# An LSTM step with the output gate's sigmoid apart, the first half's f·c apart, and ScalarE's scale factor held in a register

## The chip, the cores and the metric

One core of one Trainium2 chip runs the kernel. The time is the device time of one execution in microseconds (us). 2701.34 us is the median of three runs of the kernel before.

## The reference

A residual LSTM over 32 sequences of 512 steps, with 512 inputs and 512 hidden units. `Wx` and `Wh` are 512 x 2048, the bias has 2048 values, and all of it is float32:

```python
xW = jnp.einsum('ntd,dg->ntg', x, Wx) + b
c0 = jnp.zeros_like(h0)

def step(carry, xw_t):
    prev_h, prev_c = carry
    a = xw_t + prev_h @ Wh
    i = jax.nn.sigmoid(a[:, :Hd])
    f = jax.nn.sigmoid(a[:, Hd:2 * Hd])
    o = jax.nn.sigmoid(a[:, 2 * Hd:3 * Hd])
    g = jnp.tanh(a[:, 3 * Hd:])
    next_c = f * prev_c + i * g
    next_h = o * jnp.tanh(next_c)
    return ((next_h, next_c), next_h)
```

The output is x + h, for all steps. `x @ Wx` can be computed ahead of its step; `prev_h @ Wh` cannot, since it needs the h of the step before.

## The kernel before, in words

**Layout.** The batch of 32 and the four quarters of the hidden units together fill the 128 partitions: partition 32 j + b holds sequence b and the 128 hidden units of quarter j. A step's four gates for one partition are 512 values: i, f, o, g with 128 each. They are collected in one PSUM bank, `Z[s]`, where s is the step's place in a block of four. One matmul of TensorE has 32 stationary columns; four of them, one for each quarter j, run side by side in the array and fill the 128 partitions, so matmuls come in groups of four.

**Numbers.** Operands are cut into a high and a low float16 part, each scaled by a power of two. A product is then high x high, high x low and low x high. So Z comes out scaled by a factor that changes from block to block, and the gate functions undo that: they compute f(scale * Z) with `z_unscale`, one float32 that is the same in all partitions (column 3 of the tile `scales[:, r]`, made by VectorE in `scale_block`, L626).

**The input part** is computed two steps at a time, by a scheme that needs seven products where eight would be the plain number. TensorE does three and a half of these in each step (`third_products` and `first_product` in even steps, `second_products` and `last_product` in odd ones), six groups of 256 columns to a product, hence 21 groups a step. ScalarE and VectorE prepare the operands and move partial sums (`take_p5`, `set_c21`, `set_c11`, `cut_x_hi`, `set_c12`, `set_run`, `set_extra` on ScalarE; `add_extra`, `cut_x_lo`, `turn_x`, the forms, `scale_block` on VectorE).

**The recurrent part** (`recurrent_part`, L383) is 12 groups of 512 columns: first those of the high part of h, chunks 0 and 1 once `hT_hi_done` says that the first half of h is there, chunks 2 and 3 with the second half, then those of the low part once `hT_lo_done` says so. Its last matmul raises `z_done`.

**Order on TensorE** (L399): the recurrent part of step t, then the 21 groups of input products for later steps, then the recurrent part of t+1. While TensorE does the 21 groups, ScalarE and VectorE turn Z into the new h:

- ScalarE, `step` (L493): for each half a of the 128 hidden units of a partition, one sigmoid over i, f and o (L499, 3 x 64 values) and one tanh over g (L501, 64 values); then for each half, once c is there, tanh of c (L505). All gate functions take `z_unscale`, a 128 x 1 tile, as their scale, except in step 0, whose Z is not scaled: there the scale is the constant 1.0.
- VectorE, `step` (L751): `products(t, 0)` (L745: i g and f c of the first half in one instruction over 2 x 64 values, for which c and tanh g stand side by side in the tile `gc`), `new_c(t, 0)` (L749), `products(t, 1)`, `high_part_of_h(t, 0)` (L733: o * h_scale * tanh c), `new_c(t, 1)`, `turn_high_part(t, 0)` (L738, a transposition that writes `hT_hi`), `high_part_of_h(t, 1)`, `turn_high_part(t, 1)`. Then h in float32 (L763), the low part of h (L765) and its transposition (L768), the output sum (L775), and the work for later input products.

Each engine works through its own list in the order written; semaphores tie the lists together, and nothing reorders them. Once a block, at the end of s = 3, ScalarE copies the next block's factor into `z_unscale` (`set_z_unscale`, L489, copy in L491). SP issues all loads and stores; POOL only shares the maximum of x over partitions (L816).

There are 128 blocks of four steps. Blocks 0 and 1 and the last six are written out in the lists of ScalarE, VectorE, POOL and SP, with a loop over pairs of blocks between them; TensorE loops over single blocks. In the last steps the input products run out, since no later steps need them.

Of the kernel before, what the change touches and what calls it, by code (L numbers as in the profile page):

```python
# [6 lines left out]
F32 = mybir.dt.float32  # L7
# [3 lines left out]
ALU = mybir.AluOpType  # L11
ACT = mybir.ActivationFunctionType
# [3 lines left out]
def lstm_residual(nc, x, h0, Wx, Wh, bias, out):  # L16
# [12 lines left out]
    P = 128  # L29
    NJ = H // P  # L30
    C = P
# [18 lines left out]
    with ctx:  # L50
        def sb(name, shape, dt=F32):
            return ctx.enter_context(nc.sbuf_tensor(name, shape, dt))

        def bank(name):
            return ctx.enter_context(nc.psum_tensor(name, [P, 512], F32))

        def sem(name):
            return ctx.enter_context(nc.semaphore(name))
# [27 lines left out]
        act = sb("act", [P, ZW])  # L86

        gc = sb("gc", [P, 2, 2, C // 2])
        igfc = sb("igfc", [P, 2, 2, C // 2])
# [24 lines left out]

        scales = sb("scales", [P, 2, 4], I32)
        h_scale = sb("h_scale", [P, 1])
        z_unscale = sb("z_unscale", [P, 1])


        Z = [bank(f"Z{s}") for s in range(TB)]  # L120
# [34 lines left out]
        xfield_n_done = sem("xfield_n_done")  # L155
        zs_done = sem("zs_done")
        scales_done = sem("scales_done")
        h_scale_set = sem("h_scale_set")
        z_unscale_set = sem("z_unscale_set")
        x_turned = sem("x_turned")  # L160
# [25 lines left out]

        z_done = sem("z_done")
        sig_done = sem("sig_done")
        tanh_g_done = sem("tanh_g_done")
        igfc_done = sem("igfc_done")  # L190
        c_done = sem("c_done")
        tanh_c_done = sem("tanh_c_done")
# [19 lines left out]
        def half(tile, a):  # L212
            return tile[:, a * HC:(a + 1) * HC]

        def half_gates(tile, a):
            return tile.rearrange("p (g a c) -> p a g c", g=4, a=2)[:, a]
# [29 lines left out]
        def started(value):  # L246
            return not isinstance(value, int) or value > 0
# [183 lines left out]
        def _(sc):  # L431
# [50 lines left out]
            def take_p5(q, e):  # L482
# [3 lines left out]
                    sc.wait_ge(c22_set, q - 1)  # L486
                nc.scalar.copy(p5[:, :], extra[e][:, 0:HW]).then_inc(p5_taken, 1)

            def set_z_unscale(n, r):  # L489
                sc.wait_ge(scales_done, n + 1)  # L490
                nc.scalar.copy(z_unscale[:, :], scales[:, r, 3:4].bitcast(F32)).then_inc(z_unscale_set, 1)  # L491

            def step(t, n, s):  # L493
                if s == 0:
                    sc.wait_ge(z_unscale_set, n + 1)
                scale = 1.0 if isinstance(t, int) and t == 0 else z_unscale[:, :]
                sc.wait_ge(z_done, t + 1)
                for a in range(2):
                    nc.scalar.activation(half_gates(act, a)[:, 0:3], half_gates(Z[s], a)[:, 0:3],  # L499
                                         ACT.Sigmoid, scale=scale).then_inc(sig_done, 1)  # L500
                    nc.scalar.activation(gc[:, a, 0], half_gates(Z[s], a)[:, 3],  # L501
                                         ACT.Tanh, scale=scale).then_inc(tanh_g_done, 1)
                for a in range(2):
                    sc.wait_ge(c_done, 2 * t + 1 + a)
                    nc.scalar.activation(half(tanh_c, a), gc[:, a, 1], ACT.Tanh).then_inc(tanh_c_done, 1)  # L505
# [40 lines left out]
            set_run(2, 0, 1)  # L546
            set_extra(2, 0, 1)
            set_z_unscale(0, 0)

            def block(i, n, r):  # L550
                for s in range(TB):
                    step(n * TB + s, n, s)
                    if s == 0:
                        if within(2 * n + 1, NQ):
# [22 lines left out]
                    if s == 3:  # L577
                        if within(2 * n + 4, NQ):
                            cut_x_hi(2 * n + 4, n + 2, r, 0)
                        if within(2 * n + 3, NQ):  # L580
                            set_c12(2 * n + 3, 1)
                        if within(2 * n + 4, NQ):
                            set_run(2 * n + 4, 0, r)
                            set_extra(2 * n + 4, 0, r)
                        if within(n + 1, NB):
                            set_z_unscale(n + 1, 1 - r)
# [4 lines left out]
        def _(v):  # L591
# [109 lines left out]
            def prepare():  # L701
                nc.vector.memset(gc[:, :, 1], 0.0).then_inc(c_cleared, 1)
                turn_x(0, 0, 1)
                v.wait_ge(bias_loaded, 16 * NJ)
                nc.vector.tensor_tensor(bias_d[:, :], bias_bc[:, HW:], bias_bc[:, 0:HW], ALU.subtract).then_inc(bias_d_done, 1)
                turn_x(1, 1, 1)
                weight_scale(0)
                v.wait_ge(h0_loaded, 16 * NJ)
                nc.vector.transpose(h0_T[:, :, :], h0_in[:, :].rearrange("p (ch l) -> p ch l", ch=NCH)).then_inc(h0_turned, 1)
                for place, (k, _) in enumerate(W_ORDER):  # L710
                    cut_wx_lo(k, place)
                weight_scale(1)
                scale_tables()
                scale_block(0, 0)
                scale_block(1, 1)
                set_h_scale(0, 0)
                first_forms(0, 0)
                last_forms(0, 0)
                cut_wh_lo(0)
                cut_x_lo(1, 0, 1)  # L720
                cut_wh_lo(1)
                first_forms(1, 1)
                last_forms(1, 1)
                cut_wh_lo(2)
                cut_wh_lo(3)
                turn_x(2, 0, 2)

                cut_x_lo(2, 1, 0)
                scale_block(2, 0)

            def high_part_of_h(t, a):
                v.wait_ge(tanh_c_done, 2 * t + 1 + a)
                nc.vector.scalar_tensor_tensor(half(h_hi, a), half_gates(act, a)[:, 2], h_scale[:, :], half(tanh_c, a),  # L733
                                               ALU.mult, ALU.mult).then_inc(h_hi_done, 1)

            def turn_high_part(t, a):
                v.wait_ge(h_hi_done, 2 * t + 1 + a)
                nc.vector.transpose(hT_hi[:, NCH // 2 * a:NCH // 2 * (a + 1), :],  # L738
                                    half(h_hi, a).rearrange("p (ch l) -> p ch l", l=L)).then_inc(hT_hi_done, 1)

            def products(t, a):

                v.wait_ge(sig_done, 2 * t + 1 + a)
                v.wait_ge(tanh_g_done, 2 * t + 1 + a)
                nc.vector.tensor_tensor(igfc[:, a], half_gates(act, a)[:, 0:2], gc[:, a], ALU.mult).then_inc(igfc_done, 1)  # L745

            def new_c(t, a):
                v.wait_ge(igfc_done, 2 * t + 1 + a)
                nc.vector.tensor_tensor(gc[:, a, 1], igfc[:, a, 1], igfc[:, a, 0], ALU.add).then_inc(c_done, 1)  # L749

            def step(t):  # L751
                products(t, 0)
                new_c(t, 0)
                products(t, 1)
                high_part_of_h(t, 0)
                new_c(t, 1)
                turn_high_part(t, 0)
                high_part_of_h(t, 1)
                turn_high_part(t, 1)
                if started(t):  # L760

                    v.wait_ge(y_done, t)
                nc.vector.tensor_tensor(h32[:, :], act[:, 2 * C:3 * C], tanh_c[:, :], ALU.mult).then_inc(h32_done, 1)  # L763
                v.wait_ge(h32_done, t + 1)
                nc.vector.scalar_tensor_tensor(h_lo[:, :], h32[:, :], h_scale[:, :], h_hi[:, :],  # L765
                                               ALU.mult, ALU.subtract).then_inc(h_lo_done, 1)
                v.wait_ge(h_lo_done, t + 1)
                nc.vector.transpose(hT_lo[:, :, :], h_lo[:, :].rearrange("p (ch l) -> p ch l", ch=NCH)).then_inc(hT_lo_done, 1)  # L768
# [90 lines left out]
```

## Time and profile before

| | us |
|---|---|
| runs (3) | 2698.51, 2701.34, 2701.63; median 2701.34 |
| the profiled execution, its time | 2700.78 |
| its span, first to last instruction | 2699.0 |
| TensorE matmuls busy | 2611.6 (97%) |
| VectorE busy | 2150.0 (80%) |
| ScalarE busy | 1694.0 (63%) |
| POOL busy | 72.4 (3%) |
| mean granted TensorE clock, share of full speed | 0.988 |

What lies outside of the span is 1.8 us. The profiled execution is 0.56 us faster than the median of the three runs. Matmul ends are modelled in such a profile and neighbouring matmuls overlap, so TensorE's 97% is not to be taken as 97% at its peak; the starts of the groups say more.

### The profile page before, as it was taken

The page shows a single profiled execution, that of the slowest core. Times are in us where ns is not written, and L with a number is a line of the kernel's source. Part 1 is how long each engine was busy: PE and PEld are TensorE (multiplying, and loading weights), DVE is VectorE, ACT ScalarE, POOL GpSimd, SP SyncE. Part 2 cuts the span into 40 slices and gives each one's busy share as a digit, 9 for nine tenths or more (in the row PEclk, how much of TensorE's full clock was granted, in tenths as well). Part 3 has the DMA queues.
Part 4 walks back from the last instruction along what each step waited for, and adds up shares of the span by engine and source line. Part 5 has one row for each costly group of instructions (what it writes and reads, how often), then busy time and mean ns, then how long its engine had stood idle before and what let it go on. Part 6 is the DMA issues. An engine that isn't in the chain of part 4 may idle for free.

```text
span 2699.0 us, 163151 instructions
## 1 busy us (share of the span) xinstructions
PE 2611.6 (97%) x67528; PEld 1755.8 (65%) x67528; DVE 2150.0 (80%) x8259; ACT 1694.0 (63%) x5392; POOL 72.4 (3%) x138
## 2 busy tenths in 40 slices
PE   3599999999999999999999999999999999999998
PEld 0366666666666666666666666666666666666665
DVE  4888888888888888888888888888888888888876
ACT  2566666666666666666666666666666666666664
POOL 3000000000000000000000000000000000000000
PEclk7799999999999999999999999999999999999999
DMA  6011111111111111111111111111111111111111
GB/s 149 18 40 43 35 39 43 35 39 43 35 39 43 35 39 43 35 39 43 35 39 43 35 39 43 35 39 43 35 38 43 35 39 43 35 39 43 35 35 25
DMA packets 223517, 109.85 MB, mean 41 GB/s; under 512 B 25216, under 2 KB 222464, under 8 KB 222464
## 3 DMA queue, kind: packets, MB, share of 16 engines
q1 hardware_dynamic: 223488, 109.48, 16.2%
q8 instruction: 16, 0.26, 0.0%
q14 instruction: 13, 0.11, 0.0%
HBM read 75.83 MB, written 33.55 MB: 41 GB/s over the span
## 4 chain that ended last, share of the span: by engine, by line
PE 95%; DVE 1%; ACT 1%; issue 0%; DVEq 0%; ACTq 0%
PE Z L318 71%; PE run L318 18%; PE extra L318 6%; DVE wh_lo L681 0%; DVE gc L749 0%; ACT act L499 0%; DVE igfc L745 0%; DVE h_hi L733 0%; ACT tanh_c L505 0%; ACT wh_hi L524 0%; ACT gc L501 0%; DVE hT_hi L738 0%; DVE x_lo L615 0%; DVE zs L634 0%; DVE h_lo L765 0%
## 5 line engine op out<-in xcount | busy, mean ns | idle before, releaser
L318 PE MATMUL Z<-wh_hi,hT_hi 128*32 128x512 f16 x8176 | 801.5, 382 | 7.6 <-DVE hT_hi L738 6.4
L499 ACT ACTIVATE act<-Z,z_unscale 128x192 f32<-128x192 f32 x1022 | 431.1, 422 | 583.0 <-PE Z L318 583.0
L318 PE MATMUL Z<-wh_lo,hT_hi 128*32 128x512 f16 x8176 | 796.2, 379 | 0.0
L318 PE MATMUL Z<-wh_hi,hT_lo 128*32 128x512 f16 x8176 | 529.7, 379 | 0.0
L745 DVE TENSOR_TENSOR igfc<-act,gc 128x128 f32<-128x128 f32 x1024 | 299.6, 293 | 285.0 <-ACT gc L501 284.6
L318 PE MATMUL run<-wx_hi,x_hi 128*32 128x256 f16 x6120 | 433.1, 273 | 44.5 <-DVE x_lo L615 42.3
L505 ACT ACTIVATE tanh_c<-gc 128x64 f32<-128x64 f32 x1024 | 262.4, 256 | 339.3 <-DVE gc L749 339.3
L318 PEld LDWEIGHTS Z<-wh_hi,hT_hi 128*32 128x32 f16 x8176 | 214.6, 95 | 352.1 <-DVE hT_hi L738 234.8
L318 PE MATMUL run<-wx_lo,x_hi 128*32 128x256 f16 x6120 | 433.2, 273 | 0.0
L318 PE MATMUL run<-wx_hi,x_lo 128*32 128x256 f16 x6120 | 433.2, 273 | 0.0
L318 PE MATMUL Z<-wx_lo,x_hi 128*32 128x256 f16 x6120 | 432.8, 273 | 0.0
L318 PE MATMUL Z<-wx_hi,x_lo 128*32 128x256 f16 x6120 | 432.8, 273 | 0.0
L318 PE MATMUL Z<-wx_hi,x_hi 128*32 128x256 f16 x6120 | 432.8, 273 | 0.0
L733 DVE SCALAR_TENSOR_TENSOR h_hi<-act,h_scale,tanh_c 128x64 f16<-128x64 f32 x1024 | 291.8, 285 | 120.2 <-ACT tanh_c L505 85.9
L318 PEld LDWEIGHTS Z<-wh_hi,hT_lo 128*32 128x32 f16 x8176 | 215.4, 96 | 225.8 <-DVE hT_lo L768 113.5
L501 ACT ACTIVATE gc<-Z,z_unscale 128x64 f32<-128x64 f32 x1022 | 322.3, 315 | 0.0
L318 PEld LDWEIGHTS Z<-wh_lo,hT_hi 128*32 128x32 f16 x8176 | 218.4, 97 | 133.0 <-issue 0.7
L738 DVE STREAM_TRANSPOSE hT_hi<-h_hi 128x64 f16<-128x64 f16 x1024 | 247.6, 242 | 17.8
L749 DVE TENSOR_TENSOR gc<-igfc 128x64 f32<-128x64 f32 x1024 | 226.9, 222 | 17.4
L318 PEld LDWEIGHTS run<-wx_hi,x_hi 128*32 128x32 f16 x6120 | 164.1, 97 | 104.2 <-issue 41.6
L318 PEld LDWEIGHTS run<-wx_lo,x_hi 128*32 128x32 f16 x6120 | 164.1, 97 | 57.5
L765 DVE SCALAR_TENSOR_TENSOR h_lo<-h,h_scale,h_hi 128x128 f16<-128x128 f32 x512 | 180.3, 352 | 18.1
(88 smaller groups left out, 3586.6 us busy)
## 6 DMA issues: line engine op xcount, KB each, us to landing
x_in<-in_x SPq DMA_DIRECT2D x512, 64.0 KB, 2.1
x_res<-in_x SPq DMA_DIRECT2D x512, 64.0 KB, 2.1
out_y<-y SPq DMA_DIRECT2D x512, 64.0 KB, 1.7
wx_raw<-in_Wx SPq DMA_DIRECT2D x16, 256.0 KB, 9.1
wh_raw<-in_Wh SPq DMA_DIRECT2D x16, 256.0 KB, 20.0
bias_bc<-in_bias SPq DMA_DIRECT2D x4, 64.0 KB, 2.1
h_in<-in_h SPq DMA_DIRECT2D x4, 16.0 KB, 14.1
```

The source lines that it names most:

```text
L318: return nc.tensor.matmul(out, lhsT, rhs, start=False, stop=last, skip_group_check=True)
L499: nc.scalar.activation(half_gates(act, a)[:, 0:3], half_gates(Z[s], a)[:, 0:3], ACT.Sigmoid, scale=scale).then_inc(sig_done, 1)
L501: nc.scalar.activation(gc[:, a, 0], half_gates(Z[s], a)[:, 3], ACT.Tanh, scale=scale).then_inc(tanh_g_done, 1)
L505: nc.scalar.activation(half(tanh_c, a), gc[:, a, 1], ACT.Tanh).then_inc(tanh_c_done, 1)
L733: nc.vector.scalar_tensor_tensor(half(h_hi, a), half_gates(act, a)[:, 2], h_scale[:, :], half(tanh_c, a), ALU.mult, ALU.mult).then_inc(h_h ...
L738: nc.vector.transpose(hT_hi[:, NCH // 2 * a:NCH // 2 * (a + 1), :], half(h_hi, a).rearrange("p (ch l) -> p ch l", l=L)).then_inc(hT_hi_don ...
L745: nc.vector.tensor_tensor(igfc[:, a], half_gates(act, a)[:, 0:2], gc[:, a], ALU.mult).then_inc(igfc_done, 1)
L749: nc.vector.tensor_tensor(gc[:, a, 1], igfc[:, a, 1], igfc[:, a, 0], ALU.add).then_inc(c_done, 1)
L765: nc.vector.scalar_tensor_tensor(h_lo[:, :], h32[:, :], h_scale[:, :], h_hi[:, :], ALU.mult, ALU.subtract).then_inc(h_lo_done, 1)
```

## The change

ScalarE's sigmoid over i, f and o of a half becomes one over i and f alone (2 x 64 values). The sigmoid of o is one instruction over both halves (128 values) behind the four others, with a semaphore of its own, `sig_o_done`, that VectorE waits for ahead of the first `high_part_of_h`. On VectorE, i g and f c of the first half become two instructions: f c waits for the sigmoid alone, i g for the tanh of g. The second half stays as it was. The tile `z_unscale` becomes a register of ScalarE, loaded once a block from partition 0 of `scales`; the gate functions name the register as their scale.

```diff
@@ semaphores @@
+        scales_seen = sem("scales_seen")
...
+        sig_o_done = sem("sig_o_done")
...
+        fc_done = sem("fc_done")
+        ig_done = sem("ig_done")
@@ ScalarE @@
+            z_unscale = sc.alloc_register("z_unscale")
+
             def set_z_unscale(n, r):
                 sc.wait_ge(scales_done, n + 1)
-                nc.scalar.copy(z_unscale[:, :], scales[:, r, 3:4].bitcast(F32)).then_inc(z_unscale_set, 1)
+                sc.sem_inc(scales_seen, 1)
+                sc.reg_load(z_unscale, scales[0:1, r, 3:4]).then_inc(z_unscale_set, 1)
 
             def step(t, n, s):
-                if s == 0:
-                    sc.wait_ge(z_unscale_set, n + 1)
-                scale = 1.0 if isinstance(t, int) and t == 0 else z_unscale[:, :]
+                scale = 1.0 if isinstance(t, int) and t == 0 else z_unscale
                 sc.wait_ge(z_done, t + 1)
                 for a in range(2):
-                    nc.scalar.activation(half_gates(act, a)[:, 0:3], half_gates(Z[s], a)[:, 0:3],
+                    nc.scalar.activation(half_gates(act, a)[:, 0:2], half_gates(Z[s], a)[:, 0:2],
                                          ACT.Sigmoid, scale=scale).then_inc(sig_done, 1)
                     nc.scalar.activation(gc[:, a, 0], half_gates(Z[s], a)[:, 3],
                                          ACT.Tanh, scale=scale).then_inc(tanh_g_done, 1)
+
+                nc.scalar.activation(act[:, 2 * C:3 * C], Z[s][:, 2 * C:3 * C],
+                                     ACT.Sigmoid, scale=scale).then_inc(sig_o_done, 1)
@@ VectorE @@
             def high_part_of_h(t, a):
+                if a == 0:
+                    v.wait_ge(sig_o_done, t + 1)
                 v.wait_ge(tanh_c_done, 2 * t + 1 + a)
...
-            def products(t, a):
...
-            def new_c(t, a):
...
+            def first_products(t):
+
+                v.wait_ge(sig_done, 2 * t + 1)
+                nc.vector.tensor_tensor(igfc[:, 0, 1], half_gates(act, 0)[:, 1], gc[:, 0, 1], ALU.mult).then_inc(fc_done, 1)
+                v.wait_ge(tanh_g_done, 2 * t + 1)
+                nc.vector.tensor_tensor(igfc[:, 0, 0], half_gates(act, 0)[:, 0], gc[:, 0, 0], ALU.mult).then_inc(ig_done, 1)
+
+            def first_c(t):
+                v.wait_ge(fc_done, t + 1)
+                v.wait_ge(ig_done, t + 1)
+                nc.vector.tensor_tensor(gc[:, 0, 1], igfc[:, 0, 1], igfc[:, 0, 0], ALU.add).then_inc(c_done, 1)
+
+            def last_products(t):
+
+                v.wait_ge(sig_done, 2 * t + 2)
+                v.wait_ge(tanh_g_done, 2 * t + 2)
+                nc.vector.tensor_tensor(igfc[:, 1], half_gates(act, 1)[:, 0:2], gc[:, 1], ALU.mult).then_inc(igfc_done, 1)
+
+            def last_c(t):
+                v.wait_ge(igfc_done, t + 1)
+                nc.vector.tensor_tensor(gc[:, 1, 1], igfc[:, 1, 1], igfc[:, 1, 0], ALU.add).then_inc(c_done, 1)
 
             def step(t):
-                products(t, 0)
-                new_c(t, 0)
-                products(t, 1)
+                first_products(t)
+                first_c(t)
+                last_products(t)
                 high_part_of_h(t, 0)
-                new_c(t, 1)
+                last_c(t)
                 turn_high_part(t, 0)
```

## Rows read from the trace of the kernel before

**Rows 1.** The page's first part: busy us, share of span and instructions of each engine
```profile
PE 2611.6 (97%) x67528; PEld 1755.8 (65%) x67528; DVE 2150.0 (80%) x8259; ACT 1694.0 (63%) x5392; POOL 72.4 (3%) x138
```
**Rows 2.** Critical chain in order of time, two pieces: start us, us, what
```profile
161.30 3.42 PE Z L318 x72
...
2560.35 3.42 PE Z L318 x72
```
**Rows 3.** Timeline, TensorE, one step: start us, us, engine, line, op, out<-in, count
```profile
1300.79 0.40 PE L318 MATMUL Z<-wh_hi,hT_hi 128*32 128x512 f16 x4
...
1303.39 0.28 PE L318 MATMUL run<-wx_hi,x_hi 128*32 128x256 f16 x4
...
1305.57 0.28 PE L318 MATMUL Z<-wx_hi,x_lo 128*32 128x256 f16 x4
...
1305.85 0.40 PE L318 MATMUL Z<-wh_hi,hT_hi 128*32 128x512 f16 x4
```
**Rows 4.** Waits, longest in total: engine, line, waited for, us in total, times, longest
```profile
PEld Z L318 <- DVE hT_hi L738: 234.8, 1010, 2.8
```
**Rows 5.** Timeline, ScalarE and VectorE, the chain between two recurrent parts
```profile
1303.62 0.42 ACT L499 ACTIVATE act<-Z,z_unscale 128x192 f32<-128x192 f32 x1 [1.29 <-PE Z L318]
...
1303.93 0.31 ACT L501 ACTIVATE gc<-Z,z_unscale 128x64 f32<-128x64 f32 x1
...
1304.34 0.29 DVE L745 TENSOR_TENSOR igfc<-act,gc 128x128 f32<-128x128 f32 x1 [0.73 <-ACT gc L501]
...
1304.67 0.23 DVE L749 TENSOR_TENSOR gc<-igfc 128x64 f32<-128x64 f32 x1
...
1304.93 0.26 ACT L505 ACTIVATE tanh_c<-gc 128x64 f32<-128x64 f32 x1 [0.17 <-DVE gc L749]
...
1305.22 0.28 DVE L733 SCALAR_TENSOR_TENSOR h_hi<-act,h_scale,tanh_c 128x64 f16<-128x64 f32 x1
...
1305.56 0.24 DVE L738 STREAM_TRANSPOSE hT_hi<-h_hi 128x64 f16<-128x64 f16 x1
```
**Rows 6.** Timeline, weight loads for h's second high half and its low part
```profile
1306.58 0.10 PEld L318 LDWEIGHTS Z<-wh_hi,hT_hi 128*32 128x32 f16 x4 [0.18 <-DVE hT_hi L738]
...
1307.49 0.64 PEld L318 LDWEIGHTS Z<-wh_hi,hT_lo 128*32 128x32 f16 x16 [0.23 <-DVE hT_lo L768]
```
**Rows 7.** Timeline, ScalarE in step 0, whose scale is the constant 1.0
```profile
101.33 0.33 ACT L499 ACTIVATE act<-Z 128x192 f32<-128x192 f32 x1
101.55 0.22 ACT L501 ACTIVATE gc<-Z 128x64 f32<-128x64 f32 x1
101.66 0.34 ACT L499 ACTIVATE act<-Z 128x192 f32<-128x192 f32 x1
```
**Rows 8.** Timeline, VectorE in step 0: two instructions that wait for nothing
```profile
103.48 0.22 DVE L749 TENSOR_TENSOR gc<-igfc 128x64 f32<-128x64 f32 x1
103.62 0.28 DVE L745 TENSOR_TENSOR igfc<-act,gc 128x128 f32<-128x128 f32 x1
```
**Rows 9.** Timeline, ScalarE in a step with s = 3, and the next step's start
```profile
1293.50 0.42 ACT L499 ACTIVATE act<-Z,z_unscale 128x192 f32<-128x192 f32 x1 [1.29 <-PE Z L318]
...
1295.85 0.63 ACT L458 ACTIVATE x_hi<-forms 128x512 f16<-128x512 f32 x1
...
1297.09 0.46 ACT L468 ACTIVATE extra<-bias_d,scales 128x256 f32<-128x256 f32 x1
1297.49 0.17 ACT L491 COPY z_unscale<-scales 128x1 f32<-128x1 f32 x1
1298.56 0.42 ACT L499 ACTIVATE act<-Z,z_unscale 128x192 f32<-128x192 f32 x1 [0.89 <-PE Z L318]
```
**Rows 10.** Timeline, VectorE: its last instruction of the same step
```profile
1298.69 0.22 DVE L640 SCALAR_TENSOR_TENSOR scales<-scale_mul,zs,scale_add 128x4 int32<-128x4 int32 x1
```
**Rows 11.** DMA issues: issue line, count, KB each, us to landing
```profile
x_in<-in_x SPq DMA_DIRECT2D x512, 64.0 KB, 2.1
...
out_y<-y SPq DMA_DIRECT2D x512, 64.0 KB, 1.7
```
**Rows 12.** Timeline, TensorE in the last step, with no input products left
```profile
2688.63 0.40 PE L318 MATMUL Z<-wh_hi,hT_hi 128*32 128x512 f16 x4 [2.28 <-DVE hT_hi L738]
```

More of the change, by code:

```diff
@@ L116, in lstm_residual @@
         h_scale = sb("h_scale", [P, 1])
-        z_unscale = sb("z_unscale", [P, 1])
         Z = [bank(f"Z{s}") for s in range(TB)]
@@ L739, in turn_high_part @@
                                     half(h_hi, a).rearrange("p (ch l) -> p ch l", l=L)).then_inc(hT_hi_done, 1)
-            def products(t, a):
-                v.wait_ge(sig_done, 2 * t + 1 + a)
-                v.wait_ge(tanh_g_done, 2 * t + 1 + a)
-                nc.vector.tensor_tensor(igfc[:, a], half_gates(act, a)[:, 0:2], gc[:, a], ALU.mult).then_inc(igfc_done, 1)
-            def new_c(t, a):
-                v.wait_ge(igfc_done, 2 * t + 1 + a)
-                nc.vector.tensor_tensor(gc[:, a, 1], igfc[:, a, 1], igfc[:, a, 0], ALU.add).then_inc(c_done, 1)
+            def first_products(t):
[14 more added lines that the diff above has]
+                nc.vector.tensor_tensor(gc[:, 1, 1], igfc[:, 1, 1], igfc[:, 1, 0], ALU.add).then_inc(c_done, 1)
             def step(t):
-                products(t, 0)
-                new_c(t, 0)
-                products(t, 1)
+                first_products(t)
+                first_c(t)
+                last_products(t)
                 high_part_of_h(t, 0)
-                new_c(t, 1)
+                last_c(t)
                 turn_high_part(t, 0)
```

## The prediction

> **What bounds the kernel now.** The page's first part comes first: TensorE shows 97% busy, VectorE 80%, ScalarE 63% [rows 1], which looks as if only less matmul work could help. The critical chain in order of time gives the beat: from 161.30 to 2560.35 us lie 474 steps, so one step takes 2399.05 / 474 = 5.061 us, without drift [rows 2]. The third view, the timeline of one step, shows what fills this beat, by starts and not by ends. The recurrent part starts at 1300.79 and the input products at 1303.39, 2.60 us for its 12 groups. The 21st group of products starts at 1305.57, hence 2.18 / 20 = 0.109 us a group, and the last is through its turn at 1305.68. The next recurrent part starts at 1305.85 [rows 3]. So TensorE stands still for 0.17 us in each step: 2.60 + 2.29 + 0.17 = 5.06. The model of the matmul ends hides this hole, but the waits name what ends it: the weight load of the recurrent part waits for the transposed first half of h, 1010 times in the sum for both halves [rows 4].
>
> So the beat is a loop of latencies: Z complete, gate functions, c, tanh c, high part of h, its transposition, and TensorE's 12 groups again. Counted from ScalarE's start at 1303.62 [rows 5]: tanh of g ends at 0.62, the products start at 0.72, c at 1.05, tanh c at 1.31, h_hi at 1.60, the transposition at 1.94, and the recurrent part at 2.23. From there to ScalarE's next start are the other 2.83 of the 5.06 us (12 groups, the last one's end, the signal). A microsecond saved in the 2.23 shortens the step until TensorE's own 2.60 + 2.29 = **4.89 us** bounds it, and no further.
>
> Does the second half, or the low part, hold the loop instead? Their weight loads take 0.10 us each and start just in time for the next group [rows 6]; they have next to no slack, but they follow h_hi of the first half in VectorE's order at fixed distances. What comes earlier ahead of that h_hi brings them forward by as much.
>
> **The register as scale.** No row shows a scale from a register. The nearest rows bound it: a scale from a 128 x 1 tile (0.42 us for 192 values, 0.31 for 64 [rows 5]) and the constant of step 0 (0.33 and 0.22 [rows 7]), 0.09 less. Starts also follow closer: 0.32 behind the 192 values with the tile, 0.22 with the constant, and 0.11 behind the 64. I take the constant's value, since a register, like a constant, needs no read of 128 partitions, and these are rows of the same instructions. The tile's price stays as the other end. The Trainium skill (ScalarE: Activation LUTs, What ACT_TABLE_LOAD costs) says that immediate scale and bias take 186 ns + 0.833 ns a value and each pointer operand some 93 ns more; the trace agrees (0.09 us, and (0.33 - 0.22) / 128 = 0.86 ns a value), but neither page nor trace has the register's case. By the rule the constant's sum below would hold if the register counts as an immediate.
>
> **The sigmoid over i and f alone** spares 64 x 0.86 ns = 0.05 us ahead of the tanh of g. With the constant's durations: first sigmoid 0 to 0.28; tanh of g from 0.17 to 0.40 (0.62 before).
>
> **f c apart.** An instruction of VectorE with one wait starts 0.03 us behind what it waits for (h_hi behind tanh c), one with two waits of which the second comes last 0.10 (the products behind tanh g) [rows 5]. f c has one: it starts at 0.31. Two independent instructions, the first of 64 values, start 0.14 apart [rows 8], so i g starts at 0.45 (tanh g would allow 0.43). It takes 0.22, as c's sum over 64 values does [rows 5], where both products together took 0.29; it ends at 0.67. The sum for c now has two waits: 0.77 to 0.99. Tanh c: 1.02 to 1.28.
>
> **Sigmoid of o behind.** ScalarE's five starts are 0.17, 0.11, 0.17, 0.11 and 0.17 apart, so it is free for tanh c at 0.73, and o is there at 0.56 + 0.28 = 0.84; both are early. h_hi has two waits now: 1.28 + 0.10 = 1.38, where it was 1.60. **The loop is 0.22 us shorter**: 4.84. The second half's products need VectorE from about 0.87 on for 0.29 us, done before 1.38. What was paid for the extra waits (0.07 twice) and f c's own instruction is in this sum.
>
> TensorE's 4.89 is longer than 4.84, by a thin 0.05. **So TensorE bounds the step, and each full step gives back 0.17 of the 0.22.**
>
> **What else must keep up.** ScalarE with s = 3: x_hi starts 2.35 us behind the step's start, when TensorE's products end (their last group starts at 1305.57, 1.95 behind ScalarE's start, and takes 0.28 [rows 3, 5]), and the last copy ends at 1297.55, 4.05 behind the start [rows 9]. This part hangs on TensorE and doesn't come earlier. The register load must fit between 4.05 and 4.89, 0.84 us; what is queued behind it is the next step's first sigmoid, and behind that everything. Nothing in the trace is a register load: below it is bounded by the copy that it replaces, 0.17 us [rows 9], above by a DMA, 1.7 to 2.1 us to its landing [rows 11]. I take it as covered, because it reads one word that lies in the core's own memory, as the copy does, and no 64 KB. The Trainium skill (DMA: Bandwidth & Descriptors, Latency and other measured facts) gives a tensor_load a floor of about 600 ns, which would fit; the same skill (Runtime: NRT & Kernel Launch, the preamble breakdown) has about 1.3 us for register loads from HBM, which would not: by it 0.46 us would stand out. No run here shows either.
>
> VectorE with s = 3 has its longest list: L640 starts at 1298.69, 3.59 behind that step's h_hi and 0.13 behind the next step's start [rows 9, 10]. It comes at 1.38 + 3.59 = 4.97 of a step of 4.89, so at 0.08 of the next, and f c is wanted at 0.31: covered. SP and POOL get nothing new; the stores hang on y, which comes earlier with the step.
>
> **The sum.** 502 full steps x 0.17 = 85.3. In the last six or so the products thin out, TensorE waits up to 2.28 us for h [rows 12], and each gets the whole 0.22: 1.3. Together 86.6, less something for the loop branch of TensorE, of which no row was read: 86. Against the profiled execution's own 2700.8 that gives 2615 us; the median of the runs shown is 0.6 higher, so a median might be 2615.5. **Predicted: 2615 us**, 3.2% less.
>
> **The rivals.**
> *The register costs what the tile did.* Then tanh of g ends at 0.27 + 0.31 = 0.58, i g at 0.83, c at 1.15; but five starts (0.27 and 0.20 apart, the tile's 0.32 less 0.05 and the constant's 0.11 with 0.09 more) keep ScalarE busy to 1.21, and o's sigmoid becomes the wait ahead of tanh c. h_hi starts at 1.57, 0.03 earlier: 15 us, 2685. For it: the instruction form is unseen. Against: nothing must be fetched from 128 partitions. 6%.
> *Some of the price only.* A few hundredths for each of five gate functions, or a wait dearer than counted, and the loop of 4.84 rises over 4.89; 0.05 more costs 25 us beyond the slack. 2630 to 2655, around 2640. 12%, for the slack is thin.
> *The load holds ScalarE* (the slower side). Place: the end of s = 3, in front of the next block's first sigmoid. It costs (load - 0.84) for 127 blocks; from 0.84 + 86 / 127 = 1.52 us on the kernel is slower than before. At a DMA's 2.1 us: 1.26 x 127 = 160, hence 2775. For it: a DMA needs that long. Against: one word, no queue. 5%. At 1.3 us by the page named above it would be 0.46 x 127 = 58, 2673; 4%.
> *The floor is lower or the hole isn't there.* The hole could belong to TensorE's own change from products to the recurrent part, and then nothing is gained: 2700. The waits speak against it [rows 4]. 3%. The forecast keeps 70%.
>
> **How the numbers follow.** The forecast's own range is 2604 (0.19 us a step, if the first group of the recurrent part loses its late weight load as well) to 2629 (0.14). To hold 8 in 10 the range takes in the partial price: 2604 to 2655. What a measurement of this kernel can tell from no change is 0.2%, 5.4 us. Faster by more than that: forecast, partial price, tile's price, load at 1.3 us, 0.92. Same: 0.03. Slower: 0.05.
>
> **What would show it.** Right: a step of 4.89 us over hundreds of steps; gate functions at 0.28 (128 values) and 0.22; h_hi 1.38 behind the sigmoid's start; the products' last group and the recurrent part 0.11 apart; PEld waiting less for hT_hi. Wrong: gate functions at 0.37 and 0.31, tanh c waiting for nothing but ScalarE's own queue; a step of s = 0 longer than the others, with ScalarE idle between L468 and the sigmoid and TensorE waiting behind it; or a step of 4.89 that TensorE spends with a hole in it.

## The result, and the profile after

The changed kernel takes **2627.91 us** (median of 4 runs, 2626.70 to 2628.84) against 2700.64 for the kernel before (also 4 runs). The ratio is 0.9731, with a 95% interval of 0.9715 to 0.9748: 72.7 us less. The forecast was 2615, within 2604 to 2655.

The page of the changed kernel, busy time of each engine, the counterpart of [rows 1] (PE is TensorE, PEld its weight loads, DVE VectorE, ACT ScalarE):

```profile
PE 2534.0 (97%) x67528; PEld 1769.6 (67%) x67528; DVE 2176.8 (83%) x8771; ACT 1528.8 (58%) x5776; POOL 72.4 (3%) x138
```

TensorE does the same 67528 matmuls, and its share still reads 97%: this number was as blind to the hole as to its closing. The wait that ended the hole is the better witness. The waits of the changed kernel, the counterpart of [rows 4]:

```profile
PEld Z L321 <- DVE hT_hi L747: 62.4, 251, 2.6
```

234.8 us in 1010 waits became 62.4 in 251. In the timeline of TensorE, one plain step of the changed kernel shows it directly (counterpart of [rows 3]):

```profile
1301.07 0.39 PE L321 MATMUL Z<-wh_hi,hT_hi 128*32 128x512 f16 x4
...
1305.84 0.28 PE L321 MATMUL run<-wx_hi,x_lo 128*32 128x256 f16 x4
1305.95 0.39 PE L321 MATMUL Z<-wh_hi,hT_hi 128*32 128x512 f16 x4
```

The last group of products and the recurrent part are 0.11 us apart, one group's turn, where they were 0.28. The step is 4.88 us (the seven from 577.33 to 611.52, below, take 34.19). The chain in between, ScalarE and VectorE of the same step (counterpart of [rows 5]):

```profile
1303.88 0.28 ACT L503 ACTIVATE act<-Z 128x128 f32<-128x128 f32 x1 [0.83 <-PE Z L321]
1304.06 0.22 ACT L505 ACTIVATE gc<-Z 128x64 f32<-128x64 f32 x1
...
1304.92 0.26 ACT L512 ACTIVATE tanh_c<-gc 128x64 f32<-128x64 f32 x1 [0.18 <-DVE gc L760]
...
1304.01 0.22 DVE L647 SCALAR_TENSOR_TENSOR scales<-scale_mul,zs,scale_add 128x4 int32<-128x4 int32 x1
1304.20 0.23 DVE L753 TENSOR_TENSOR igfc<-act,gc 128x64 f32<-128x64 f32 x1
1304.34 0.22 DVE L755 TENSOR_TENSOR igfc<-act,gc 128x64 f32<-128x64 f32 x1
1304.66 0.23 DVE L760 TENSOR_TENSOR gc<-igfc 128x64 f32<-128x64 f32 x1
...
1305.28 0.29 DVE L742 SCALAR_TENSOR_TENSOR h_hi<-act,h_scale,tanh_c 128x64 f16<-128x64 f32 x1
```

The gate functions have the constant's durations, 0.28 and 0.22, and h_hi starts 1.40 us behind the first sigmoid, 1.60 before; 1.38 was forecast.

Some 505 steps (half of the 1010 waits of [rows 4]) at 0.178 less would give 90 us, more than the 72.7 measured. What is missing lies in one step of eight. The same engines around 614 us, where the loop of VectorE turns over:

```profile
614.34 0.28 ACT L503 ACTIVATE act<-Z 128x128 f32<-128x128 f32 x1 [0.84 <-PE Z L321]
...
614.48 0.22 DVE L647 SCALAR_TENSOR_TENSOR scales<-scale_mul,zs,scale_add 128x4 int32<-128x4 int32 x1
615.01 0.23 DVE L753 TENSOR_TENSOR igfc<-act,gc 128x64 f32<-128x64 f32 x1 [0.32 <-ACT act L503]
...
615.48 0.23 DVE L760 TENSOR_TENSOR gc<-igfc 128x64 f32<-128x64 f32 x1
...
616.10 0.28 DVE L742 SCALAR_TENSOR_TENSOR h_hi<-act,h_scale,tanh_c 128x64 f16<-128x64 f32 x1
```

From the start of L647 to that of f c (L753) are 0.53 us here and 0.19 in the plain case above, which is the same place in the other block of the loop; there f c waits for the sigmoid and not for L647. The idle time here is put down to the sigmoid too, but that ended at 614.62. What stands between is seen only in the view of the loop's own line, L261, in this stretch (DVEq is VectorE's sequencer; number, shortest/median/longest in ns, first and last start):

```profile
L261 DVEq COMPARE_BRANCH x1: 56/56/56, 614.6 to 614.6; - x1
L261 DVEq FUSED_REGOPS x1: 85/85/85, 614.9 to 614.9; - x1
```

The sequencer branches back and computes its registers, with 0.3 us from the one's start to the other's; what fills that time is in no view. f c starts 0.67 us behind the first sigmoid instead of 0.31. h_hi comes at 1.76, and TensorE waits. Its recurrent parts there:

```profile
577.33 0.40 PE L321 MATMUL Z<-wh_hi,hT_hi 128*32 128x512 f16 x4
...
611.52 0.40 PE L321 MATMUL Z<-wh_hi,hT_hi 128*32 128x512 f16 x4
...
616.73 0.40 PE L321 MATMUL Z<-wh_hi,hT_hi 128*32 128x512 f16 x4
```

The last two are 5.21 us apart, and the eight steps from 577.33 to 616.73 take 39.40, 0.34 more than 8 x 4.883. 60 loop turns of that are some 20 us, as read from the trace; the run with the branch moved, below, measures 16.8.

### The profile page after: what moved, and what is told of

It reads as the page before. It is cut to its first block, busy times and chain, and to the rows that moved or that the text cites. A ratio compares the mean times of both kernels' runs of the same rounds, so it can differ in the third digit from the quotient of the medians.

```text
span 2625.3 us, 164755 instructions
## 1 busy us (share of the span) xinstructions
PE 2534.0 (97%) x67528; PEld 1769.6 (67%) x67528; DVE 2176.8 (83%) x8771; ACT 1528.8 (58%) x5776; POOL 72.4 (3%) x138
## 4 chain that ended last, share of the span: by engine, by line
PE 68%; DVE 20%; issue 4%; ACT 4%; DVEq 1%; ACTq 0%
PE Z L321 53%; PE run L321 12%; PE extra L321 4%; DVE h_hi L742 3%; ACT tanh_c L512 3%; DVE h_lo L786 2%; DVE gc L760 2%; DVE igfc L755 2%; DVE hT_hi L747 2%; DVE x_lo L622 1%; DVE y L796 1%; DVE gc L770 1%; DVE igfc L753 1%; DVE h L784 1%; DVE Z L628 1%
## 5 line engine op out<-in xcount | busy, mean ns | idle before, releaser
L503 ACT ACTIVATE act<-Z 128x128 f32<-128x128 f32 x1024 | 287.2, 281 | 558.4 <-PE Z L321 558.4
L321 PEld LDWEIGHTS Z<-wh_hi,hT_hi 128*32 128x32 f16 x8176 | 214.7, 95 | 256.0 <-DVE hT_hi L747 62.4
L505 ACT ACTIVATE gc<-Z 128x64 f32<-128x64 f32 x1024 | 235.9, 230 | 0.0
L753 DVE TENSOR_TENSOR igfc<-act,gc 128x64 f32<-128x64 f32 x512 | 115.6, 226 | 109.2 <-ACT act L503 93.6
L461 ACT ACTIVATE x_hi<-forms 128x512 f16<-128x512 f32 x255 | 160.6, 630 | 58.1 <-PE Z L321 58.1
```

Of the source, the lines that this page charges most:

```text
L321: return nc.tensor.matmul(out, lhsT, rhs, start=False, stop=last, skip_group_check=True)
L461: nc.scalar.activation(x_hi[:, e], forms_of_pair(r, e), ACT.Copy).then_inc(x_hi_cut, 1)
L503: nc.scalar.activation(half_gates(act, a)[:, 0:2], half_gates(Z[s], a)[:, 0:2], ACT.Sigmoid, scale=scale).then_inc(sig_done, 1)
L753: nc.vector.tensor_tensor(igfc[:, 0, 1], half_gates(act, 0)[:, 1], gc[:, 0, 1], ALU.mult).then_inc(fc_done, 1)
```

## The experiments

Times are compared with the kernel before, run beside each group of experiments (medians of 2699.8 to 2701.6 us), or with the changed kernel's 2627.9.

**The scale back in the tile.** In the changed kernel:

```diff
-            z_unscale = sc.alloc_register("z_unscale")
+        z_unscale = sb("z_unscale", [P, 1])
...
-                sc.reg_load(z_unscale, scales[0:1, r, 3:4]).then_inc(z_unscale_set, 1)
+                nc.scalar.copy(z_unscale[:, :], scales[:, r, 3:4].bitcast(F32)).then_inc(z_unscale_set, 1)
...
-                scale = 1.0 if isinstance(t, int) and t == 0 else z_unscale
+                scale = 1.0 if isinstance(t, int) and t == 0 else z_unscale[:, :]
```

> The changed kernel with its scale factor in the 128 x 1 tile again. Theory A (the register is what brings the gain, since gate functions of 128 values drop from 0.37 to 0.28 us and the queue of five from 1.21 to 0.73 us; the two splits alone bring 0.03 us a step): tanh c waits for ScalarE's own queue, h_hi starts near 1.57 us behind the first sigmoid, a step takes 5.03 us and every eighth one some 0.2 us more, in all about 2695 us, no more than 15 us below the kernel before. Theory B (the splits bring at least half of the gain): 2665 us or less.

Measured: 2685.77 us (2684.70 to 2687.53), ratio 0.9946 (0.9931 to 0.9961). Theory A. Its timeline, ScalarE and VectorE:

```profile
1301.91 0.37 ACT L502 ACTIVATE act<-Z,z_unscale 128x128 f32<-128x128 f32 x1 [0.95 <-PE Z L321]
1302.18 0.31 ACT L504 ACTIVATE gc<-Z,z_unscale 128x64 f32<-128x64 f32 x1
...
1302.82 0.39 ACT L507 ACTIVATE act<-Z,z_unscale 128x128 f32<-128x128 f32 x1
1303.11 0.26 ACT L511 ACTIVATE tanh_c<-gc 128x64 f32<-128x64 f32 x1
...
1303.47 0.28 DVE L741 SCALAR_TENSOR_TENSOR h_hi<-act,h_scale,tanh_c 128x64 f16<-128x64 f32 x1
```

Tanh c (L511) has no idle time ahead of it: ScalarE's queue holds it, at 1.20 us, and h_hi comes at 1.56. A plain step takes 5.01 us, somewhat less than expected, and the step at the loop branch 5.21. With the tile the two splits are worth 15 us, and the register on top of them the other 58. That holds for this order alone: the next run takes the register first.

**The register alone.** In the kernel before, the register in place of the tile and nothing else (the first diff read the other way round):

> The kernel before with the register as scale and nothing else changed. Theory A: tanh of g ends 0.44 us behind the first sigmoid's start, the products start at 0.54, h_hi at 1.41; the loop of 4.87 us is under TensorE's own 4.883, so TensorE bounds the step here too. At VectorE's loop branch, once in eight steps, the products start near 0.73 and the step is 0.2 us longer (60 times, 12 us). About 2617 us, some 10 us below the changed kernel. Theory B (each part of the change adds to the gain): clearly over 2628 us, 2645 or more.

Measured: 2619.53 us (2617.88 to 2619.84), ratio 0.9701 (0.9688 to 0.9715). Theory A, and less than the whole change takes. Its timeline at VectorE's loop branch:

```profile
612.10 0.33 ACT L500 ACTIVATE act<-Z 128x192 f32<-128x192 f32 x1 [0.83 <-PE Z L318]
...
612.84 0.29 DVE L746 TENSOR_TENSOR igfc<-act,gc 128x128 f32<-128x128 f32 x1 [0.39 <-ACT act L500]
...
613.71 0.28 DVE L734 SCALAR_TENSOR_TENSOR h_hi<-act,h_scale,tanh_c 128x64 f16<-128x64 f32 x1
```

The branch holds this kernel too, its products starting at 0.74, but from there to h_hi are 0.87 us, against 1.09 from f c to h_hi in the changed kernel: there is no second product instruction, one wait less ahead of the sum, and one less ahead of h_hi. The eight steps to the recurrent part behind it take 39.24 us (575.10 to 614.34), so the long one is 5.06 if the other seven are at TensorE's 4.883.

**The branch moved.** In the changed kernel, VectorE's loop is cut behind the work of s = 0, and the instructions on data and their order stay:

```diff
-            def block(i, n, r):
-                for s in range(TB):
+            def block(i, n, r, steps=range(4)):
+                for s in steps:
...
-            run_blocks(v, block)
+            last = NB // BODY
+            block(0, 0, 0)
+            block(0, 1, 1)
+            block(1, 2, 0, (0,))
+            with v.Fori(1, last - 3) as i:
+                block(i, i * BODY, 0, (1, 2, 3))
+                block(i, i * BODY + 1, 1)
+                block(i + 1, i * BODY + 2, 0, (0,))
+            block(last - 3, (last - 3) * BODY, 0, (1, 2, 3))
+            block(last - 3, (last - 3) * BODY + 1, 1)
+            for i in range(last - 2, last):
+                for r in range(BODY):
+                    block(i, i * BODY + r, r)
```

> The changed kernel with VectorE's loop cut at another place: its branch stands behind the work of a step with s = 0 (the shortest list) in place of s = 3 (the longest). No instruction on data is added or taken away. Theory A (the eighth step of 5.20 us is VectorE's branch, which puts f c 0.67 us behind the first sigmoid's start where 0.31 was wanted): all steps take 4.88 us, 60 x 0.31 = 19 us less, 2609 us. Rival (the long step belongs to ScalarE's branch, to the register load or to TensorE's own loop): the long step stays, 2628 us.

Measured: 2611.06 us (2609.93 to 2611.39), ratio 0.9668 (0.9655 to 0.9681). Theory A. Eight recurrent parts on TensorE, with the loop's turn among them:

```profile
600.72 0.39 PE L321 MATMUL Z<-wh_hi,hT_hi 128*32 128x512 f16 x4
...
639.81 0.39 PE L321 MATMUL Z<-wh_hi,hT_hi 128*32 128x512 f16 x4
```

39.09 us, 4.886 a step. The long step is gone, and the 16.8 us between this kernel and the changed one are shown to be the branch's place. Of the 20 us read from the trace 2 are not won, since a step here is still 0.003 over 4.883; the rest is within what the runs scatter.

**The branch moved in the kernel before.** The same edit there, as a control:

> The kernel before with VectorE's loop branch behind the work of s = 0, and nothing else. Theory A (the branch cost nothing before the change, since the first products were wanted 0.72 us behind the sigmoid's start and the branch let them go at 0.70): the steps stay at 5.06 us and the time within 2 us of the kernel before. Rival (the branch cost time in the kernel before too): 10 to 19 us less.

Measured: 2700.33 us (2699.22 to 2701.15), ratio 0.9999 (0.9990 to 1.0009). Theory A. The branch cost nothing that can be measured before the change; it was covered by the very latency that the register took away.

**Both products of the first half whole again.** In the changed kernel:

```diff
                 v.wait_ge(sig_done, 2 * t + 1)
-                nc.vector.tensor_tensor(igfc[:, 0, 1], half_gates(act, 0)[:, 1], gc[:, 0, 1], ALU.mult).then_inc(fc_done, 1)
                 v.wait_ge(tanh_g_done, 2 * t + 1)
-                nc.vector.tensor_tensor(igfc[:, 0, 0], half_gates(act, 0)[:, 0], gc[:, 0, 0], ALU.mult).then_inc(ig_done, 1)
+                nc.vector.tensor_tensor(igfc[:, 0], half_gates(act, 0)[:, 0:2], gc[:, 0], ALU.mult).then_inc(ig_done, 1)
...
-                v.wait_ge(fc_done, t + 1)
```

> The changed kernel with i g and f c of the first half in one instruction again (128 values, waiting for sigmoid and tanh), o and the register as changed. Theory A: products at 0.49 us, c at 0.81 against 0.78 with f c apart (the sum for c has one wait again), h_hi at 1.42; the loop of 4.88 us is at TensorE's 4.883, nothing is lost in a plain step. At VectorE's branch one instruction less stands between it and c: c near 1.03 in place of 1.13, so that the long step shrinks by 0.1 us, 60 x 0.1 = 6 us: 2622 us. Rival (f c apart carries its 0.07 us in full): a step of 4.93 us, 2645 to 2650 us.

Measured: 2635.28 us (2633.70 to 2636.88), ratio 0.9759 (0.9745 to 0.9772). Neither. Theory A had the sign wrong: without f c apart the kernel loses 7 us where it was to win 6. The plain step is 4.893, so the loop of latencies is now 0.01 us over TensorE's floor, some 5 us in all: h_hi comes at 1.44 and not at the 1.42 expected. The step at the branch is 5.14, 0.06 less than in the changed kernel, where 0.1 was expected. And one step in eight, away from the branch, takes 4.99. ScalarE and VectorE in that step:

```profile
588.19 0.28 ACT L502 ACTIVATE act<-Z 128x128 f32<-128x128 f32 x1 [0.84 <-PE Z L320]
...
588.78 0.29 DVE L753 TENSOR_TENSOR igfc<-act,gc 128x128 f32<-128x128 f32 x1 [0.43 <-ACT act L502]
```

The products start 0.59 us behind the sigmoid and not at 0.49, with VectorE idle. What holds them for that 0.1 us (6 us in all) stays open; no run was made for it.

**The sigmoid of o back with i and f**, f c apart and the register as changed:

```diff
-                    nc.scalar.activation(half_gates(act, a)[:, 0:2], half_gates(Z[s], a)[:, 0:2],
+                    nc.scalar.activation(half_gates(act, a)[:, 0:3], half_gates(Z[s], a)[:, 0:3],
                                          ACT.Sigmoid, scale=scale).then_inc(sig_done, 1)
...
-                nc.scalar.activation(act[:, 2 * C:3 * C], Z[s][:, 2 * C:3 * C],
-                                     ACT.Sigmoid, scale=scale).then_inc(sig_o_done, 1)
...
-                if a == 0:
-                    v.wait_ge(sig_o_done, t + 1)
```

> The changed kernel with the sigmoid of o back in those of i and f (192 values), so that h_hi waits for tanh c alone; f c apart and the register as changed. Theory A: in a plain step nothing changes, 4.883 us, since TensorE bounds it. At VectorE's branch the front of the chain is given by the branch, and h_hi starts 0.03 us behind tanh c in place of 0.10, so the long step shrinks from 5.20 to 5.13 us: 60 x 0.07 = 4 us, 2624 us. Rival (o behind carries its 0.05 us ahead of tanh g in the long step too): 5.20 us or more, 2628 us or more.

Measured: 2620.76 us (2619.55 to 2621.22), ratio 0.9706 (0.9692 to 0.9719). Theory A in sign, and twice its size: eight steps take 39.26 us (575.75 to 615.01), so the long one is 5.08 and not 5.13. The split of o costs 7 us where it stands. The branch in this run:

```profile
612.75 0.33 ACT L502 ACTIVATE act<-Z 128x192 f32<-128x192 f32 x1 [0.83 <-PE Z L320]
...
612.83 0.22 DVE L643 SCALAR_TENSOR_TENSOR scales<-scale_mul,zs,scale_add 128x4 int32<-128x4 int32 x1
613.37 0.23 DVE L747 TENSOR_TENSOR igfc<-act,gc 128x64 f32<-128x64 f32 x1 [0.31 <-ACT act L502]
...
614.38 0.28 DVE L736 SCALAR_TENSOR_TENSOR h_hi<-act,h_scale,tanh_c 128x64 f16<-128x64 f32 x1
```

From f c to h_hi are 1.01 us, 0.08 less than in the changed kernel. And f c itself starts 0.62 us behind its sigmoid, where the changed kernel has 0.67. These 0.05 come from the step before, whose h_hi starts VectorE's list down to the branch. First the changed kernel's, then this run's:

```profile
609.46 0.28 ACT L503 ACTIVATE act<-Z 128x128 f32<-128x128 f32 x1 [1.33 <-PE Z L321]
...
610.89 0.28 DVE L742 SCALAR_TENSOR_TENSOR h_hi<-act,h_scale,tanh_c 128x64 f16<-128x64 f32 x1
```

```profile
607.87 0.33 ACT L502 ACTIVATE act<-Z 128x192 f32<-128x192 f32 x1 [1.34 <-PE Z L320]
...
609.25 0.29 DVE L736 SCALAR_TENSOR_TENSOR h_hi<-act,h_scale,tanh_c 128x64 f16<-128x64 f32 x1
```

h_hi comes 1.43 us behind the sigmoid there and 1.38 here, and from it to L647 or L643 are 3.59 and 3.58.

**The register alone, with the branch moved:**

> The register alone, with VectorE's loop branch behind the work of s = 0, as in the run with the branch moved. Theory A (TensorE bounds every step once the branch is out of the way, and neither split of the change is then needed): all steps 4.883 us, the eighth 0.17 us shorter than with the register alone, 60 x 0.17 = 10 us less than 2619.5, so 2609 us, the same as the changed kernel with the branch moved (2611) within 3 us. Rival (the splits still carry something, as the loop of 4.88 us with the products whole is at TensorE's 4.883): 2615 us or more.

Measured: 2608.97 us (2606.96 to 2612.18), ratio 0.9664 (0.9651 to 0.9677). Theory A. This is the lowest median of the study (single runs overlap with those of the changed kernel with its branch moved), with one instruction less a step than the changed one on VectorE and one less on ScalarE. From

```profile
599.61 0.39 PE L318 MATMUL Z<-wh_hi,hT_hi 128*32 128x512 f16 x4
...
638.67 0.39 PE L318 MATMUL Z<-wh_hi,hT_hi 128*32 128x512 f16 x4
```

eight steps take 39.06 us, 4.883 each. TensorE bounds every one.

**What the register load costs.** Two kernels tried to repeat it. Six loads of the one register in a row:

> The changed kernel with six loads of the register in a row in place of one. One load showed 0.28 us and stood in the trace beside copies that are ahead of it in ScalarE's program. Theory A (loads pass beside the work that is queued, from about 2.5 us behind a step's start on, and six take some 2.1 us, which end before the next step): no change, 2628 us, at most 5 more. Rival (a load waits its turn behind the last copy, at 4.05 us, with 0.84 us of room): six take 2.1 us, 1.26 us too long, 127 times, 2785 us.

Measured: 2629.56 us (2627.73 to 2629.68). That tells nothing: the trace holds 128 loads, one a block, as the changed kernel's does. Loads whose value was overwritten before use were no longer in the program. The same with a signal behind each load:

> Six loads of the register in a row again, each with its own signal now, since only one load a block stood in the trace of the run before it. Theory A (loads pass beside the queued work, and six of 0.28 us with some 0.07 between them take 2.1 us from 2.5 us behind the step's start, 4.6 in a step of 4.88): no more than 5 us over the changed kernel's 2628. Rival (a load waits behind the last copy at 4.05 us): 1.26 us too long, 127 times, 2785 us.

Measured: 2636.11 us (2635.26 to 2638.12), 8 us over the changed kernel, and again 128 loads; the other five became signals alone, so it tells nothing of loads either. (Its step at the branch is 5.32 us. VectorE's wait for the register, which counts six a block now, was changed with it; that this makes the 0.12 us wasn't tried.) What remained was to use every load: five registers, one for each gate function of a step.

```diff
-            z_unscale = sc.alloc_register("z_unscale")
+            z_unscale = [sc.alloc_register(f"z_unscale{k}") for k in range(5)]
...
-                sc.reg_load(z_unscale, scales[0:1, r, 3:4]).then_inc(z_unscale_set, 1)
+                for reg in z_unscale:
+                    load = sc.reg_load(reg, scales[0:1, r, 3:4])
+                load.then_inc(z_unscale_set, 1)
...
-                                         ACT.Sigmoid, scale=scale).then_inc(sig_done, 1)
+                                         ACT.Sigmoid, scale=scale[2 * a]).then_inc(sig_done, 1)
```

> The changed kernel with a register of its own for each of the five gate functions of a step, so that each block needs five loads that are all used. Theory A (loads pass beside the queued work from 2.5 us behind the step's start, 0.35 us each, 1.75 in all, done at 4.3 of 4.88): within 5 us of the changed kernel's 2628. Rival (loads wait behind the last copy, room 0.84 us): 0.91 us too long, 127 times, 2743 us.

Measured: 2630.27 us (2627.38 to 2631.70), within 2.4 us of the changed kernel. Theory A. The trace has 640 loads, five a block.

> The same with ten registers, five for even and five for odd steps. Theory A: ten loads of 0.35 us take 3.5 us from 2.5 on and end at 6.0, 1.1 us into the next step: 127 times 1.1 us more, 2770 us. Rival (loads wait behind the last copy): 2.7 us too long, 127 times, 2965 us.

Measured: 2751.44 us (2749.89 to 2752.89), ratio 1.0187 (1.0170 to 1.0204). Theory A, with the loads shorter than assumed. The view of the load's line in one block of it, then ScalarE around it and the recurrent parts on either side:

```profile
L498 ACTq TENSOR_LOAD <-scales x10: 273/276/436, 1299.1 to 1302.1; - x10
```

```profile
1296.56 0.28 ACT L506 ACTIVATE act<-Z 128x128 f32<-128x128 f32 x1 [1.33 <-PE Z L321]
...
1299.45 0.37 ACT L479 COPY Z<-run 128x256 f32<-128x256 f32 x1
...
1300.16 0.46 ACT L471 ACTIVATE extra<-bias_d,scales 128x256 f32<-128x256 f32 x1
1302.84 0.28 ACT L506 ACTIVATE act<-Z 128x128 f32<-128x128 f32 x1 [2.22 <-issue]
```

```profile
1298.63 0.40 PE L321 MATMUL Z<-wh_hi,hT_hi 128*32 128x512 f16 x4
...
1304.86 0.40 PE L321 MATMUL Z<-wh_hi,hT_hi 128*32 128x512 f16 x4 [1.16 <-DVE hT_hi L750]
```

The first load starts at 1299.1, ahead of the starts of three instructions that stand before it in the program (L479, L466 and L471); they go on beside the loads. The last ends at some 1302.4, and the next sigmoid, whose input had been ready, starts at 1302.84, with 2.22 us of idle time put down to "issue". Between the two stands ScalarE's own loop branch, which is covered in the changed kernel:

```profile
L261 ACTq COMPARE_BRANCH x1: 45/45/45, 1302.5 to 1302.5; - x1
L261 ACTq FUSED_REGOPS x1: 59/59/59, 1302.7 to 1302.7; - x1
```

The step lasts 6.23 us instead of the changed kernel's 5.2. In a block without the branch it is 5.82 (1319.52 to 1325.34 for the recurrent part) instead of 4.89. In the changed kernel the one load looks like this:

```profile
L497 ACTq TENSOR_LOAD <-scales x1: 276/276/276, 1301.5 to 1301.5; - x1
```

0.28 us, over at 1301.8, and the next sigmoid starts at 1303.88: 2.1 us to spare.

## Why the prediction was right, and where it was 13 us off

**The bound.** Right: a loop of latencies with a hole of 0.17 us on TensorE, and a floor of 4.89 (4.883 measured: the first recurrent group no longer starts behind a late weight load). The recurrent part itself takes 2.59 us in the timeline of the changed kernel (1301.07 to the products' start at 1303.66), 2.60 before. The kernel with register and moved branch sits on this floor in every step.

**The register as scale.** Right, and it is the step that everything hung on: 0.28 and 0.22 us, the constant's price, and 2619.5 us by this edit alone. The first rival, the tile's price, was put at 2685 us; the run with the tile took 2685.8. This agreement is partly luck, since a plain step gained 0.05 there and not 0.03, and the branch took some of it back.

**The two splits.** Their sum was right in a plain step (h_hi at 1.38 forecast, 1.40 measured), but they were not asked separately whether they were needed. By the prediction's own method the register alone gives h_hi at 1.41 or 1.42 and a loop under the floor; the splits then buy slack that nobody uses in a plain step.

**What else must keep up.** This is the step that failed: "It comes at 1.38 + 3.59 = 4.97 of a step of 4.89, so at 0.08 of the next, and f c is wanted at 0.31: covered." VectorE's list was followed to L640, its last instruction on data, and not over the loop branch behind it. The instruction comes at 0.14 of the next step and not at 0.08, since h_hi of the step before is at 1.43 and not at 1.38, which alone would have cost nothing. But with the branch and the registers behind it there are 0.53 us from that instruction's start to f c, so f c starts 0.67 and not 0.31 behind the sigmoid once in eight steps. The branch at another place gives back 16.8 us, more than the whole miss of 13 us. The other way went the floor, lower by 0.007 a step (some 4 us) than the one taken. A loop branch was thought of for TensorE only, where it stayed hidden: in the kernel with register and moved branch all steps are 4.883. So the 13 us are a larger error less a smaller one. That 2628 lies just inside the forecast's own range, to 2629, is luck: this end was set for a step that gains 0.14 us everywhere, not for one long step in eight.

**The load.** Right in the sum (covered), for a wrong reason. It was placed behind the last copy, with 0.84 us of room. In fact it doesn't queue behind the copies: the changed kernel's load starts at 1301.5, ahead of the last copies, and is over 2.1 us before the sigmoid. One of the prediction's signs of being wrong, a longer step of s = 0, did appear in every second block, but the load isn't its cause, since moving VectorE's branch removed it. The Trainium skill's floor for a tensor_load, about 600 ns (DMA: Bandwidth & Descriptors, Latency and other measured facts), doesn't agree with the trace here: 0.27 us each, 0.30 from start to start, for one word from the core's own memory. The 1.3 us of the Trainium skill (Runtime: NRT & Kernel Launch, the preamble breakdown) is for register loads from HBM, which no run here has.

**Order of the parts**, as medians: kernel before 2700.6, register 2619.5, and o behind 2635.3, and f c apart 2627.9 (the change), and the branch moved 2611.1. Without o behind, f c apart stands at 2620.8, close to the register alone. So f c apart brings 7 us only where o behind has taken 16, and the whole change is 8 us slower than its register alone.

## What to carry to other kernels

When a latency on the critical loop is shortened, ask engine by engine what else was hidden under it, and follow each engine's list over its loop branch to the next instruction that matters, since a branch is in no busy time. Once another engine becomes the bound, the remaining parts of a change may buy nothing there, as here, and still pay for their extra instructions and waits where the chain is late: try each part alone. And a per-partition scale that is the same in all partitions is worth a register, if a gate function lies on the critical loop.

## What the runs showed that was not expected

- ScalarE's register load runs beside the work already queued: it started while three instructions that stand before it in the program had yet to start, took 0.27 us, and ten of them in a row 3.0 from the first's start to the last's. So "nothing reorders them", as the kernel before is described, doesn't hold for a register load.
- With a loop branch between them, VectorE's last instruction on data and the next one start 0.53 us apart, 0.34 more than at the same place without a branch, where the next one waited for something else; the branch is visible only in the line of the loop.
- An instruction that waits for two semaphores, the second of them last, starts some 0.10 us behind the end of what it waited for (h_hi behind tanh c in the changed kernel), one with a single wait 0.03 (h_hi with o back in its place). Splitting one instruction off adds such waits on both sides.
